# Eight batches through one core's matrix engine: the closes of the first batch, the halves of the adapters and the negatives of x at other steps

## What is computed

```python
# layer 0: quantise x by 8 thresholds, then a gated mixture of 4 rank-16 adapters
gi = jnp.sum(jnp.abs(x)[..., None] <= thresholds, axis=-1)
idx = jnp.minimum(gi, G - 1)
d = deltas[idx]; zp = zero_points[idx]
x_dequant = (jnp.clip(jnp.round(x / d) + zp, 0, 63) - zp) * d
h = jnp.where(gi == G, 0, x_dequant)
logits = h @ router_w.T                    # 4 experts, the best 2 kept
gates = softmax(sparse, axis=-1)
mid = jnp.einsum('tf,erf->ter', h, A)
all_deltas = jnp.einsum('ter,eor->teo', mid, B) * 4
x1 = x + jnp.einsum('te,teo->to', gates, all_deltas)
# layer 1: a dense product with a rank-32 adapter chosen per batch, and another
# dense product with two rank-32 adapters
c = x1 @ W.T + (x1 @ lora_A[labeler]) @ lora_B_w.T * 0.5
out = x1 + c @ kernel + bias + adapters(c)
```

## Time and profile before

| | us |
|---|---|
| median of 3 runs | 442.37 |
| lowest and highest run | 441.23, 444.02 |
| the profiled execution, its own time | 441.27 |
| span of the profiled execution | 439.5 |
| PE, DVE, ACT, POOL busy | 426.8, 384.3, 363.7, 59.8 |
| granted TensorE clock, mean | 0.999 |

### The profile page before, as it was taken

One profiled execution on the slowest core, in us unless ns is written; L12 is line 12 of the kernel. 1 busy time (PEld: TensorE's weight loads), 2 busy tenths in 40 slices (PEclk: granted clock), 3 DMA queues, 4 the chain that ended last, 5 costly groups with the idle time before them and its releaser, 6 DMA issues.

```text
span 439.5 us, 5658 instructions
## 1 busy us (share of the span) xinstructions
PE 426.8 (97%) x2136; PEld 341.4 (78%) x2136; DVE 384.3 (87%) x394; ACT 363.7 (83%) x314; POOL 59.8 (14%) x55
## 2 busy tenths in 40 slices
PE   8999999999999989979999999999999999999995
PEld 8877677888878878758777877787778778877873
DVE  1697979989999999999999899999999999999300
ACT  1599999938988888999989989999999998995002
POOL 0000004000040000130412213222130210330000
PEclk9999999999999999999999999999999999999999
DMA  7999539960479945370781862938870970283024
GB/s 265 352 309 408 177 85 292 197 160 0 119 244 268 274 107 195 69 183 1 172 152 23 186 175 45 210 68 182 179 172 20 191 134 1 52 153 47 9 40 95
DMA packets 40173, 66.09 MB, mean 150 GB/s; under 512 B 26994, under 2 KB 27250, under 8 KB 37874
## 3 DMA queue, kind: packets, MB, share of 16 engines
q0 software_dynamic: 8368, 38.28, 37.6%
q1 hardware_dynamic: 31778, 27.45, 21.9%
HBM read 55.23 MB, written 18.87 MB: 169 GB/s over the span
## 4 chain that ended last, share of the span: by engine, by line
PE 36%; DVE 30%; ACT 12%; issue 10%; DMA 9%; SPq 2%; ACTq 0%; DVEq 0%
DVE val L760 14%; DMA wst<-w_in 9%; PE bank L1217 8%; PE bank L1219 7%; PE bank L1218 7%; DVE val L742 6%; ACT val L484 5%; ACT level L471 4%; PE bank L1191 4%; DVE inside L751 3%; PE bank L1061 3%; PE bank L1030 2%; DVE p_lo L925 1%; DVE kp_lo L808 1%; ACT tst L617 1%
## 5 line engine op out<-in xcount | busy, mean ns | idle before, releaser
L760 DVE COPY_PREDICATED val<-inside,val 128x2048 f32<-128x2048 uint8 x56 | 143.0, 2553 | 0.3
L484 ACT ACTIVATE val<-level,shift,small 128x2048 f32<-128x2048 int16 x64 | 133.7, 2091 | 1.9 <-PE bank L1061 1.9
L471 ACT ACTIVATE level<-xq,inv 128x2048 int16<-128x2048 f32 x64 | 127.7, 1997 | 0.6
L1217 PE MATMUL bank<-p_hi,x_hi 128*128 128x512 f32 x256 | 107.4, 420 | 0.0
L1219 PE MATMUL bank<-p_hi,x_lo 128*128 128x512 f32 x256 | 100.1, 391 | 0.0
L1218 PE MATMUL bank<-p_lo,x_hi 128*128 128x512 f32 x256 | 99.9, 390 | 0.0
L742 DVE TENSOR_SCALAR val<-val,width,unshift 128x2048 f32<-128x2048 f32 x64 | 86.4, 1350 | 3.9 <-ACT val L484 3.8
L751 DVE TENSOR_SCALAR inside<-absx,thr 128x2048 uint8<-128x2048 f32 x56 | 72.2, 1290 | 0.0
L1217 PEld LDWEIGHTS bank<-p_hi,x_hi 128*128 128x128 f32 x256 | 48.1, 188 | 14.2 <-issue 5.1
L1218 PEld LDWEIGHTS bank<-p_lo,x_hi 128*128 128x128 f32 x256 | 48.1, 188 | 11.8 <-issue 3.1
L1219 PEld LDWEIGHTS bank<-p_hi,x_lo 128*128 128x128 f32 x256 | 48.1, 188 | 10.5
(11 more groups left out here) (118 smaller groups left out, 512.7 us busy)
## 6 DMA issues: line engine op xcount, KB each, us to landing
out_t<-bias_in POOLq DMA_DIRECT2D x8, 1024.0 KB, 16.9
out_t<-ost POOLq DMA_DIRECT2D x15, 512.0 KB, 7.6
wst<-w_in SPq DMA_DIRECT2D x14, 512.0 KB, 8.7
xq<-xt_in POOLq DMA_DIRECT2D x7, 1024.0 KB, 8.2
x_hi<-xt_in POOLq DMA_DIRECT2D x7, 1024.0 KB, 6.7
x_lo<-xt_in POOLq DMA_DIRECT2D x14, 512.0 KB, 6.0
la<-la_in SPq DMA_DIRECT2D x4, 512.0 KB, 5.6
kst<-k_in SPq DMA_DIRECT2D x4, 512.0 KB, 13.4
```

The source lines that it names most:

```text
L471: nc.scalar.activation(level[:, g % 2], xq[:, c % 2], ACT.Copy, scale=inv[:, group(g)]).then_inc(levels_made, 1)
L484: nc.scalar.activation(val[:, turn(c, g)], level[:, g % 2], ACT.Relu, bias=shift[:, group(g)], scale=par[:, 1, group(g)]).then_inc(raised, 1)
L760: nc.vector.copy_predicated(val[:, acc(c)], inside[:, g % 2], val[:, turn(c, g)]).then_inc(merged, 1)
L1217: mm(o, x_hi[b % 3][:, k, at], p_hi[:, h, k], start=k == 0 and n < OWN, stop=False)
```

## The change

The tables change as follows.

- CLOSE of the first batch goes from step 5 to step 6. For the last batch its rule becomes one step behind ZEND where it was two, but ZEND[7] goes from 60 to 61, so that CLOSE[7] stays at 62. Through LAGS, CLOSE[4] goes from 36 to 37 and CLOSE[6] from 53 to 55; the others stay.
- XAT goes from (0, 2) to (0, 1): the second negative a step sooner. UHAT goes from 3 to 0, ULAT from 3 to 1 and BUAT from 3 to 2.
- LAST, the step of the last quantisation group, goes from 71 to 72, counted with the first stage's 16. The groups of the main stage spread over one step more.
- LAGS change for batches 2 to 7: mid of batches 3, 5, 6 and 7 a step later; the gates of batch 3 two steps later and of batches 4 to 7 one or two; the turns of batches 2 to 7 a step later, of batch 6 two.
- TAKE[0] to TAKE[2] go from 8 to 9.
- The last tile (n = 31) gets its closing matmul between its two steps and not behind them. The other branches of `early` with `2 * n > CLOSE[b]` are never taken.
- The transfer of itok goes from SP's queue to POOL's.

```diff
--- before.py
+++ after.py
@@ -221,11 +221,11 @@
 
     ZADD = 1
     AHEAD, HOLD = 2, 2
-    LAGS = [(3, 3, 6, 7, 8, 9), (3, 3, 3, 4, 4, 6), (2, 4, 4, 6, 7, 9), (2, 3, 3, 4, 5, 6), (3, 6, 6, 7, 8, 9), (2, 3, 4, 5, 5, 7), (1, 2, 2, 4, 5, 6), (2, 2, 2, 3, 4, 5)]
+    LAGS = [(3, 3, 6, 7, 8, 9), (3, 3, 3, 4, 4, 6), (2, 4, 4, 6, 8, 9), (2, 4, 4, 5, 5, 6), (3, 6, 7, 8, 9, 10), (2, 3, 4, 5, 5, 6), (1, 2, 2, 5, 6, 7), (2, 2, 3, 3, 4, 5)]
     TAKEN = [1, 0, 1, 2, 2, 1, 1, 1, 1, 1, 1, 1, 1, 1, 1, 1, 1, 2]
     ORDER = [(c, g) for c in range(BATCH) for g in range(G)]
     SLOTS = STEPS + BATCH * KT
-    LAST = STEPS + BATCH * KT - 9
+    LAST = STEPS + BATCH * KT - 8
     rest, room = len(ORDER) - AHEAD - sum(TAKEN), LAST + 1 - len(TAKEN)
     TAKEN += [(i + 1) * rest // room - i * rest // room for i in range(room)]
     TAKEN += [0] * (SLOTS - len(TAKEN))
@@ -243,7 +243,7 @@
     OUT_AT = OUT
     OUT = {at: c for c, at in OUT_AT.items()}
 
-    XAT, UHAT, ULAT, BUAT, ZAT, ZLAT = (0, 2), 3, 3, 3, 5, 7
+    XAT, UHAT, ULAT, BUAT, ZAT, ZLAT = (0, 1), 0, 1, 2, 5, 7
 
 
     V_AT = (4, 10)
@@ -271,7 +271,7 @@
 
 
     ZEND = [max(b * KT, OUT_AT[b] - STEPS, 3) for b in range(BATCH)]
-    CLOSE = [max(b * KT + 1, ZEND[b] + HOLD) for b in range(BATCH)]
+    CLOSE = [max(b * KT + 1, ZEND[b] + (HOLD if 0 < b < BATCH - 1 else HOLD + 1 if b == 0 else 1)) for b in range(BATCH)]
     LAG = 3
     TAKE = [max(2 * q + 1, CLOSE[q // TILES]) + LAG for q in range(BATCH * TILES)]
 
@@ -338,6 +338,8 @@
                 part = slice(p * XK, (p + 1) * XK)
                 pool.wait_ge(x_neg_made, (c - 1) * XPARTS + p + 1)
                 pool.dma_start(x_lo[:, c % 2, part], x_v[c][:, part], accum_op=ALU.add).then_inc(x_lo_in, 16)
+
+            pool.dma_start(itok_sb, itok).then_inc(itok_in, 16)
 
             for c in range(1, BATCH):
                 if READ[c] < STEPS:
@@ -363,7 +365,6 @@
         @block.sync
         def _(sp):
             sp.dma_start(small, a["small"]).then_inc(small_in, 16)
-            sp.dma_start(itok_sb, itok).then_inc(itok_in, 16)
             for g in range(NG):
                 sp.dma_start(la[:, g], a["la"][:, g]).then_inc(lora_in[g], 16)
             sp.dma_start(bw, a["bw"]).then_inc(bw_in, 16)
@@ -1208,16 +1209,21 @@
                     else:
                         pe.wait_ge(taken, n - CRING + 1)
                 o, at = cols[n % CRING], slice(t * P, (t + 1) * P)
+                early = b == BATCH - 1 and 2 * n >= CLOSE[b]
+                if part == 0 and early and 2 * n > CLOSE[b]:
+                    mm(o, zt[:, b % ZSLOTS, at], tb[:, b % 2, h * HALF:(h + 1) * HALF], start=True, stop=False)
                 if part == 0 and n >= OWN:
                     if n == OWN:
                         pe.wait_ge(ones_made, 1)
                         pe.wait_ge(bias_made, 1)
-                    mm(o, ones, bias[:, h * HALF:(h + 1) * HALF], start=True, stop=False)
+                    mm(o, ones, bias[:, h * HALF:(h + 1) * HALF], start=not (early and 2 * n > CLOSE[b]), stop=False)
                 for k in range(part * KT // 2, (part + 1) * KT // 2):
-                    mm(o, x_hi[b % 3][:, k, at], p_hi[:, h, k], start=k == 0 and n < OWN, stop=False)
+                    mm(o, x_hi[b % 3][:, k, at], p_hi[:, h, k], start=k == 0 and n < OWN and not (early and 2 * n > CLOSE[b]), stop=False)
                     mm(o, x_hi[b % 3][:, k, at], p_lo[:, h, k], start=False, stop=False)
-                    last = mm(o, x_lo[:, s, k, at], p_hi[:, h, k], start=False, stop=False)
-                if j == KT - 1:
+                    last = mm(o, x_lo[:, s, k, at], p_hi[:, h, k], start=False, stop=early and k == KT - 1)
+                if early and part:
+                    last.then_inc(ofull, 1)
+                elif j == KT - 1:
                     last.then_inc(x_done, 1)
                 if q == 1:
                     z_begin(0)
@@ -1234,7 +1240,9 @@
                         pe.wait_ge(bp_copied, 1)
                     for m in range(c * TILES, min((c + 1) * TILES, (q + 1) // 2)):
                         close(m)
-                elif part and q > CLOSE[b]:
+                    if early and part == 0:
+                        mm(o, zt[:, b % ZSLOTS, at], tb[:, b % 2, h * HALF:(h + 1) * HALF], start=False, stop=False)
+                elif part and q > CLOSE[b] and not early:
                     close(n)
                 if slot(b, j) in MID:
                     mid(MID[slot(b, j)])
```

## The result

| | before | after |
|---|---|---|
| median of 4 runs, us | 443.19 | 438.75 |
| lowest and highest run | 441.23, 444.67 | 438.12, 438.94 |
| the profiled execution | 441.27 | 438.94 |
| its span | 439.5 | 437.1 |

The ratio is 0.989, with a 95% interval of 0.9857 to 0.9923: faster by 1.1%, or 4.4 us. It lies at the edge of what the bound of 1% separates. The forecast was 439.1, in a range of 437.0 to 441.4. The two profiled executions differ by only 2.33 us, though, and the medians by 4.44. Both the match and that gap need an explanation.

What follows compares the result with a forecast made beforehand. PE bounds the kernel. 2.56 + 0.79 - 0.1 - 0.3 + 0.3 = 3.25, say 3.3 us, takes the profiled execution from 441.27 to 438.0; the median, 1.1 above it, becomes 439.1, range 437.0 to 441.4.

Steps and rivals of the forecast that it cites:

- Part 1: First batch, CLOSE[0] a step later: PE's stand before the closes goes, 2.56 us gained; releasers early by 0.1 to 3 us.
- The transfer of x_lo: First batch, on POOL: lands at 191.6, 3 us early; by the skill's figure it would slip 2.5 us, to 194.1.
- Part 2: Batch 6, mid a step later and closes two: PE's wait at mid(6) goes, 0.79 us gained.
- Part 3: New waits: none at tile 5 (0.6 us to spare), 0.1 us at batch 3's turn, 0.3 allowed for gates and z_end.
- Part 4: The end: last close ahead of 12 matmuls, last batch's mid, turn and z_end a step later; 0 us.
- Part 5: The start: with itok off its queue SP issues everything else one issue sooner; 0.3 us gained, bounds 0 and 0.36.
- rival C: Spread of the runs before is varying waits that slack takes too: median 4.4 us and more lower, 437.0 to 438.0; chance 0.22.
- Rival B: A thin margin (0.1, 0.6, 0.7 us) fails on ACT or DVE; a new 1 to 2.5 us wait, 440.0 to 442.0; chance 0.20.
- rival E: First batch: bp or tb, not z_sum, released the closes; the 2.56 us come back elsewhere, about 442; chance 0.03.
- Rival D: Batch 3: DVE reaches the gates a whole group late, price 4.86 us; 1.5 slower, 443.9; chance 0.05.

Runs made afterwards that it cites:

- e2: The change itself, unedited, run again against the kernel before: median 437.80 us, ratio 0.9905, main stage 251.64 us.
- e6: The whole change but with the transfer of itok on SP's queue as before: median 438.77 us, ratio to before 0.9932.
- e11: The whole change but with the last tile's close behind its two steps as before: median 438.80 us, ratio to before 0.9903.
- e12: The whole change but with BUAT 3 instead of 2, so bu_begin stands beside z_end: median 439.40 us, ratio to before 0.9930.
- e4: The kernel before with CLOSE[0] a step later and the change's XAT, UHAT, ULAT and BUAT: median 441.33 us, ratio 0.9994.
- e8: The whole change but with CLOSE[0] at 5 as before: median 439.71 us, ratio to before 0.9963.
- e5: The kernel before with only the transfer of itok moved to POOL's queue: median 441.28 us, ratio 0.9979.
- e1: The kernel before, unedited, run again: median 442.06 us, ratio 1.0001.
- e7: The kernel before with LAGS, LAST and the last batch's part of the change alone: median 441.13 us, ratio 0.9976.
- group 1: The first of three groups of follow-up runs, beside runs of the kernel before, which took 441.92 us in the median, 441.27 at full clock.
- e3: The kernel before with only CLOSE[0] a step later: median 441.22 us, ratio 0.9993.
- e10: e4 with six unread matmuls put ahead of mid(6), where its profile waits: median 441.01 us, ratio to before 0.9954.

## Why the prediction was right, point by point

**The time** is right: 439.1 was forecast and 438.75 measured. The mechanism of the main stage is right, too. Without itok the sum was 2.95 us, and the main stage became 2.82 shorter, to 0.05 in each of the five profiles (after, e2, e6, e11, e12). But two errors in it cancel (0.7 us too much for the first batch, 0.6 too little behind it), which is luck, and a third term was not in the forecast. For the profiled execution 438.0 was forecast and 438.94 measured; 0.80 of this is the later start of its main stage.

**Part 1, the releasers: right to a tenth.** The profile of after begins its main stage 0.80 us late. With this added, DVE and ACT came where they were forecast: the second negative was made at 185.10 (184.3 + 0.8), bu was ready at 191.52 (190.6 + 0.8), the adapters' half ended at 192.58 (191.9 + 0.8), z_sum at 197.99 (197.17 + 0.8) and the merge at 201.87 (200.99 + 0.8). Every cover held. z_begin(1) came without a wait, but not near 194.4, the sign that was named, nor at 194.66 + 0.8, the sum's own value: it came at 196.26.

**Part 1, the gain: too large by 0.7 us.** It was forecast at 2.56 and is 1.85 (e4 has 1.80). The step that failed is the silence on PE's own work: I priced the places that move at what they cost before. PE's timeline in the change has bu_begin(1) and z_end(0) a step apart:

```profile
186.09 1.15 PE L1086 MATMUL bank<-ub,bet 128*64 128x64 f32 x16
187.16 0.50 PE L1221 MATMUL bank<-p_hi,x_hi 128*128 128x512 f32 x1
187.50 0.39 PE L1222 MATMUL bank<-p_lo,x_hi 128*128 128x512 f32 x1
...
190.11 0.65 PE L1114 MATMUL bank<-zt,bu 128*64 128x256 f32 x2
190.69 0.50 PE L1221 MATMUL bank<-p_hi,x_hi 128*128 128x512 f32 x1
191.02 0.39 PE L1222 MATMUL bank<-p_lo,x_hi 128*128 128x512 f32 x1
```

In the kernel before they stood beside each other, and both together delayed the next step by 1.17 us. Apart they delay it by 1.16 and 0.67, which is 0.66 more. A step's first matmul is also followed after 0.34 us and not 0.23 when it comes behind such a group, and that happens twice now and not once: 0.11 more. So PE comes to z_begin(1) 0.80 us later than in the sum (14.95 us into the main stage and not 14.15). From there to mid(2) it takes 0.09 less: 2.56 - 0.80 + 0.09 = 1.85. e12 puts the two together again and is 0.56 shorter up to mid(2), and the wait that came back in e8 is 0.9 shorter than before.

**The transfer of x_lo.** The tile's durations of issue (least, median, most, in ns) and landings in after answer to the earlier trace rows:

```profile
L340 POOL DMA_DIRECT2D x_lo<-xt_in x14: 874/901/2428, 182.9 to 380.5; - x14
...
DMA to landing us min/median/max: 5.4/6.8/8.3
```

The landings became slower, 6.8 us in the median instead of 6.0. The second of the first batch was issued at 185.40 in 0.89 us. With the slowest landing of 8.3 it is there by 193.7, and PE wants it at 196.26. By the rule of the Trainium skill, page "SBUF — State Buffer", section "SBUF: two separate sides", read as one for every instruction of VectorE, this issue would have been stretched. It was not stretched here, so its estimate of 2.5 us did not come. The traces show where it does come. Below are the two issues of the first batch in the change, a stretched one and this one, each with the instruction of DVE beside it:

```profile
182.94 1.87 POOL L340 DMA_DIRECT2D x_lo<-xt_in  x1 [9.17 <-ACT x_lo L555]
183.45 1.28 DVE L752 TENSOR_SCALAR inside<-absx,thr 128x2048 uint8<-128x2048 f32 x1
...
185.40 0.89 POOL L340 DMA_DIRECT2D x_lo<-xt_in  x1 [0.58 <-ACT x_lo L555]
184.65 2.52 DVE L761 COPY_PREDICATED val<-inside,val 128x2048 f32<-128x2048 uint8 x1
```

The long issue ends at 184.81, 0.08 us behind the end of the TENSOR_SCALAR. All 5 issues above 1 us in the kernel before, and all 6 in the change, end 0.08 to 0.13 us behind the end of a TENSOR_SCALAR. The others, 0.86 to 0.91 us long, run under a merge (COPY_PREDICATED) or other instructions, and none of them lasts to the end of a TENSOR_SCALAR. So the rule agrees with these traces where DVE runs a TENSOR_SCALAR, and the margin held because this issue fell under a merge. Why the landings became slower isn't shown.

**Part 2: right.** The bracket at mid(6) is gone. It began at 368.93 for a forecast of 368.2 + 0.8. That it came on time, though PE had gained 0.7 less in the first batch, has the same cause the other way round: z_end of batch 5 and the bu_begin behind it stand a step apart in the kernel before (0.66 and 1.16 us) and beside each other in the change (1.17). The next such pair, behind mid(6), was side by side (1.17) and is now apart, and from mid(6) to the end PE takes 0.65 more for the same work. DVE's 1.31 us are gone as well.

**Part 3: wrong on the safe side.** I took 0.1 and 0.3 us off for new waits, and none came, behind ost near 215 neither. DVE had mg at 260.67, for a forecast of 259.88 + 0.8. PE came not at 259.74 + 0.8 but at 261.64, because it had gained 0.7 less in the first batch, and the closes and small groups on the way cost it the rest. Its own lateness opened the cover. The part behind mid(2) therefore gained 0.97, for a forecast of 0.79 - 0.4.

**Part 4: right,** by e11.

**Part 5: size open.** SP's timeline in after answers to the earlier trace rows:

```profile
8.60 1.13 SPq L378 DMA_DIRECT2D wst<-w_in  x1
14.60 4.81 SPq L383 DMA_DIRECT2D alt<-alt_in  x8
```

Both come 0.61 and 0.65 us sooner than before, but this pair of profiles exaggerates. Over the 14 profiles the medians of these two starts are 8.88 and 14.82 with itok on SP (8 profiles) and 8.58 and 14.53 with it on POOL (6): 0.3 us sooner, the one issue that was forecast. PE's wait stands at 28.00 as before, with 0.6 us, and where the other profiles have it, it scatters from 27.10 to 28.30. What I named as the sign, a first wst wait 0.3 us sooner, can't be seen in that. The runs of e5 speak for more than 0.3, and no profile shows where more would come from.

**What was missing: the clock, and so rival C.** Rival C said that the spread of the runs before is waiting that varies, and that the change would take it away. But it is not the wait that varies: it is 2.35 to 2.42 us in the four profiles whose first batch is that of before (before, e1, e5, e7). What varies is whether the clock falls behind it, as it does in e1 and e5 and not in the other two. Half of the runs before are low and take 1.5 to 2.1 us more, and so their median pays near 1 us. Of the change's runs in the first comparison and in e2, 10 in all, none is low. Of the kernels with the same main stage within 0.05 us, e6, e11 and e12, 7 of 22 are low, though, 6 of these on the second chip, where the change itself wasn't run. In e11's profile the clock falls in the first stage, behind w_lo. So the change takes away one place where the clock falls, and the low runs become fewer, 7 of 32 with its own counted against 39 of 78, but they don't vanish. On the second chip alone the 6 of 15 aren't clearly fewer than the 13 of 22 of before. The sum at full clock is 3.5 us (437.79 against 441.27, group 1): 2.8 for the main stage and some 0.7 ahead of or behind it, to which itok belongs. With 0.65 for the clock in group 1, the median of before less that of its runs at full clock, it gives the 4.1 of e2. How much of the 4.4 in the first comparison is clock isn't on record run by run. That 439.1 was so close owes something to luck: the forecast left out the clock and started from a median of three runs, which the fourth put 0.8 higher.

**Rival B** acts where LAGS are left as before (e4), and rival E's moved wait where XAT to BUAT are (e3, for 2.0 us). Rival D came nowhere. In the whole change the tables take care of each other: the first batch's part alone gives 0.5 us at full clock, LAGS alone 1.2, itok alone 0.9, together 2.6, and the change 3.5. In the main stage alone the profiles say the same: 0.61 and 0.91 apart, 1.52 together, and 2.82 in the change.

## What to carry to other kernels

A wait on the engine that bounds the kernel can cost more than it lasts, since its clock may fall behind it. A kernel whose runs lie in two groups should be read run by run with the granted clock, not by its median. When the engine is moved ahead at one place, price also what its own small groups cost once they stand apart, and look for the next places where it will be early: without later work moved likewise the gain goes into the next wait. And compare stages from their own first row, when the start scatters by more than the change is worth.

## What the runs showed of the hardware that was not expected

- Behind a wait of 2.0 to 2.4 us in a stage that was otherwise full TensorE ran at half clock for 3.4 us in three profiles of five (e1, e3, e5; not in before and e7). Six records, of three float32 matmuls, took 4.10 and 4.54 us instead of 2.84.
- Behind waits of 1.89 and 2.07 us it fell as well (e10, e11), and behind one of 2.00 it did not (after).
- The main stage repeats closely: in the five profiles of the change and of the edits that don't bear on it, it is 251.60 to 251.65 us. The first stage ahead of it varies by 3 us over all profiles (178.83 to 181.91).
- Two small groups of matmuls cost PE 0.7 us less beside each other than apart (1.17 against 1.16 + 0.67), and 0.1 more is lost at each step that starts behind such a group.
- An issue of a transfer on POOL takes 0.9 us, or up to 2.8 when DVE runs a TENSOR_SCALAR meanwhile. Then it ends 0.08 to 0.13 us behind it. Under the merge (COPY_PREDICATED), which is longer, it takes 0.9.
